# Reading back the last eight tiles of partial sums by gathers that leave out the tokens without a place, and summing the tiles in another order

## The reference, cut to what matters

```python
topk_w, topk_idx = jax.lax.top_k(scores, TOP_K)          # 6 experts for each of 2048 tokens
eid = topk_idx.reshape(-1)
order = jnp.argsort(eid)                                  # stable: by expert, then by token
pos = jnp.arange(T * TOP_K) - starts[eid_s]
valid = pos < CAP                                         # each expert takes its first 64 tokens
...
out_s = jnp.where(valid[:, None], d[eid_s, pos_c], 0.0)   # everything behind them gives 0
y = jnp.einsum('tkh,tk->th', out_exp.reshape(T, TOP_K, H), topk_w)
```

## Time and profile before

| | us |
|---|---|
| median of 3 runs | 652.74 |
| lowest and highest run | 652.25, 655.45 |
| profiled execution, its own time | 653.42 |
| span of its profile (first to last instruction) | 651.7 |
| pairs, from the first gather of rows to the last put's landing | about 501 to 620.4 |
| tail, from there to the end | 31.3 |

### The profile page before, as it was taken

How to read it: one execution, slowest core, us unless ns; L and a number is a source line. 1 busy time by engine, 2 the same in 40 slices (tenths; PEclk the granted TensorE clock), 3 DMA queues, 4 the chain that set the end, 5 groups by cost and what they waited for, 6 DMA issues and landing times.

```text
span 651.7 us, 7493 instructions
## 1 busy us (share of the span) xinstructions
PE 553.4 (85%) x2367; PEld 342.9 (53%) x2367; DVE 512.6 (79%) x1182; ACT 191.0 (29%) x372; POOL 126.2 (19%) x121
## 2 busy tenths in 40 slices
PE   7467999799999869999899776749889999999764
PEld 6344666444667456674566553427565444434443
DVE  7998888264899969999999999999988466456444
ACT  2113321225443254432643305421111333223100
POOL 2120201220001100011000210000001667677600
PEclk9679999987999959999899966789999999999979
DMA  7960000327301084010730207928561699995498
GB/s 273 409 213 34 33 1 34 113 65 259 130 0 49 26 310 153 0 42 25 277 113 1 81 25 260 384 78 307 175 230 55 198 341 352 344 312 87 55 342 310
DMA packets 62741, 105.75 MB, mean 162 GB/s; under 512 B 6096, under 2 KB 51920, under 8 KB 62192
## 3 DMA queue, kind: packets, MB, share of 16 engines
q1 hardware_dynamic: 51792, 85.97, 37.4%
q0 software_dynamic: 8608, 17.21, 10.2%
q10 hardware_dynamic: 2304, 2.10, 0.9%
HBM read 79.80 MB, written 25.46 MB: 162 GB/s over the span
## 4 chain that ended last, share of the span: by engine, by line
DVE 39%; PE 25%; DMA 17%; issue 5%; ACT 4%; POOL 2%; SPq 1%; DVEq 0%; POOLq 0%; ACTq 0%
DMA part_rows<-bc,att_s 12%; DVE scan_area L1370 10%; PE gate_ps L745 6%; PE up_ps L745 5%; DVE scan_area L1373 5%; DVE scan_area L1366 5%; PE misc_ps L762 4%; DMA bc<-part_rows 3%; DVE sig L1310 2%; PE turn_ps L678 2%; DMA front_area<-sorted_dram 1%; DVE work L1460 1%; DVE front_area L1315 1%; DVE ln_st L1123 1%; PE ssm_ps L699 1%
## 5 line engine op out<-in xcount | busy, mean ns | idle before, releaser
L1370 DVE TENSOR_TENSOR_SCAN scan_area<-scan_area 128x1024 f32<-128x1024 f32 x32 | 73.3, 2292 | 4.0 <-ACT scan_area L1044 0.5
L745 PE MATMUL gate_ps<-big,front_area 128*128 x144 | 72.8, 631 | 1.4 <-ACT front_area L944 1.4
L762 PE MATMUL misc_ps<-big,front_area 128*128 x288 | 67.5, 388 | 2.4 <-ACT front_area L944 2.4
L745 PE MATMUL up_ps<-big,front_area 128*128 x144 | 68.5, 598 | 0.0
L762 PEld LDWEIGHTS misc_ps<-big,front_area 128*128 128x128 f32 x288 | 55.0, 194 | 14.1 <-issue 6.7
L980 ACT ACTIVATE sig<-gate_ps 128x512 f32<-128x512 f32 (+1 forms) x48 | 28.5, 596 | 109.9 <-PE up_ps L745 79.4
L663 POOL DMA_INDIRECT part_rows<-bc,att_s x32 | 50.4, 1576 | 22.2 <-DMA part_rows<-bc,att_s 15.8
L1310 DVE SCALAR_TENSOR_TENSOR sig<-sig,gate_ps 128x512 f32<-128x512 f32 (+1 forms) x48 | 32.7, 682 | 23.2 <-ACT sig L980 22.8
L1044 ACT ACTIVATE scan_area<-scan_area,a_col 128x511 f32<-128x511 f32 x64 | 41.9, 714 | 31.0 <-DVE scan_area L1370 27.5
L745 PEld LDWEIGHTS up_ps<-big,front_area 128*128 128x128 f32 x144 | 28.2, 196 | 36.3 <-issue 36.3
L634 POOL DMA_INDIRECT front_area<-ysorted_dram,slot_idx x16 | 20.2, 1262 | 138.3 <-DMA ysorted_dram<-front_area 134.6
(11 more groups left out here) (276 smaller groups left out, 956.5 us busy)
## 6 DMA issues: line engine op xcount, KB each, us to landing
bc<-bc_dram SPq DMA_DIRECT2D x4, 4096.0 KB, 13.7
big<-in_wgu SPq DMA_DIRECT2D x14, 704.0 KB, 8.7
part_rows<-zeros SPq DMA_DIRECT2D x16, 512.0 KB, 15.4
front_area<-in_wgu SPq DMA_DIRECT2D x6, 704.0 KB, 7.6
scan_area<-in_wgu SPq DMA_DIRECT2D x6, 704.0 KB, 9.0
big<-part_rows SPq DMA_DIRECT2D x8, 512.0 KB, 6.4
big<-in_wd SPq DMA_DIRECT2D x12, 256.0 KB, 8.5
table<-row_area SPq DMA_DIRECT2D x4, 640.0 KB, 4.2
```

Source lines behind the costliest of these rows:

```text
L745: mm = pe.matmul(bank[:], xs_t[:, k, j, :], gu0[:, expert_of[b, j], k, g, half * 512:(half + 1) * 512], start=(k == 0), stop=(k == K - 1))
L762: mm = pe.matmul(misc_ps[:, 0:D], h0_t[:, half, c * P:(c + 1) * P], dn0[:, expert_of[b, j], half * 4 + c, :], start=(half == 0 and c == 0) ...
L1370: nc.vector.tensor_tensor_scan(buf.rearrange(flat), d_a[:, g % 2, :, :].rearrange(flat), buf.rearrange(flat), 0.0, ALU.mult, ALU.add).then ...
```

## The change

Four things, all for the end of the kernel.

1. **The last eight tiles** (8 to 15) are no longer loaded by SP. During the pairs, seven small DVE instructions and two of PE work out the highest token value in the list of places (`reach`: a row-wise maximum, a transpose, a maximum over the row, a product with ones that hands it to all partitions). From it comes, for each of the 1024 late tokens, an index: its own number, or its number plus 2048 where it lies behind the last token with a place. Behind its last put POOL issues eight indirect gathers (4 KB for a token), with `bounds_check=N - 1` and no error for an index beyond it, so that such a token isn't fetched.
2. Where nothing is fetched, the area must hold zeros: DVE clears the eight late areas, one 128x1024 memset in each of the pairs 23 to 30. `parts` is laid out anew, so that these areas are free by pair 23.
3. **The order of the sums**: DVE sums tiles 1, 3, 5, 7, 13, 14, 15, PE tiles 0, 2, 4, 6, 8, 9, 10, 11, 12. The stores follow in the order in which tiles are finished.
4. **WAKE_LAST**: 20 products of zeros on PE between the shared expert and the first sum.

```diff
+WAKE_LAST = 20
 TILES = B * J
+LATE = TILES // 2
+BY_PE = [0, 2, 4, 6, 8, 9, 10, 11, 12]
+BY_DVE = [1, 3, 5, 7, 13, 14, 15]
+OUT_ORDER = [i for two in zip(BY_DVE, BY_PE) for i in two] + BY_PE[len(BY_DVE):]
+CLEAR_FROM = PAIRS - LATE - 1
...
-        parts = [mem[:, n * part_size:(n + 1) * part_size] for mem, count in ((big, 8), (front_area, 5), (area, 3))
-                 for n in range(count)]
+        parts = [mem[:, at:at + part_size]
+                 for mem, base, count in ((big, 0, 4), (front_area, 2 * part_size, 4),
+                                          (big, 2 * pair_size, 6), (front_area, 0, 2))
+                 for at in range(base, base + count * part_size, part_size)]
...
-            for i in range(TILES):
+            for i in range(LATE):
                 sp.dma_start(parts[i], part_of[i]).then_inc(part_loaded[i], 16)
...
+            pool.wait_ge(reach_steps, 7)
+            pool.wait_ge(late_clear, LATE)
+            for put in rows_put:
+                pool.wait_ge(put, 16 * PAIRS // YO_RING)
+            for n in range(LATE):
+                pool.indirect_dma_start(parts[LATE + n], None, part_of_token,
+                                        bass.IndirectOffsetOnAxis(late_idx[:, n:n + 1], 0),
+                                        bounds_check=N - 1, oob_is_err=False).then_inc(part_loaded[LATE + n], 16)
...
+                if p == 5:
+                    pe.wait_ge(reach_steps, 2)
+                    pe.transpose(up_ps[0][0:1, 0:P], reach[:, 0:1], ident[:]).then_inc(reach_turned, 1)
+                if p == 9:
+                    pe.wait_ge(reach_steps, 3)
+                    pe.matmul(up_ps[0][:, P:P + 1], ones[0:1, :], reach[0:1, 1:2], start=True, stop=True
+                              ).then_inc(reach_turned, 1)
...
+            for _ in range(WAKE_LAST):
+                pe.matmul(turn_ps[0][:, 0:D], ident[:], zeros[:, 0:D], start=True, stop=True)
-            for i in range(0, TILES, 2):
+            for n, i in enumerate(BY_PE):
                 pe.wait_ge(part_loaded[i], 16)
...
+                if p == 11:
+                    dve.wait_ge(reach_turned, 2)
+                    ts(reach[:, 2:3], up_ps[0][:, P:P + 1], -1.0, float(PER_TOKEN * N), ALU.mult, ALU.add
+                       ).then_inc(reach_steps, 1)
...
+                if CLEAR_FROM <= p < CLEAR_FROM + LATE:
+                    dve.wait_ge(down1_filled, CLEAR_FROM - 1)
+                    nc.vector.memset(parts[LATE + p - CLEAR_FROM], 0.0).then_inc(late_clear, 1)
...
-            for i in range(0, TILES, 2):
-                part, xt = parts[i + 1], x_res[:, i + 1, :]
...
+            for n, i in enumerate(BY_PE):
+                if n < len(BY_DVE):
+                    part, xt = parts[BY_DVE[n]], x_res[:, BY_DVE[n], :]
```

More of the change, by code:

```diff
@@ L276, in build @@
         part_size = PER_TOKEN * D
-        parts = [mem[:, n * part_size:(n + 1) * part_size] for mem, count in ((big, 8), (front_area, 5), (area, 3))
-                 for n in range(count)]
+        parts = [mem[:, at:at + part_size]
+                 for mem, base, count in ((big, 0, 4), (front_area, 2 * part_size, 4),
+                                          (big, 2 * pair_size, 6), (front_area, 0, 2))
+                 for at in range(base, base + count * part_size, part_size)]
+        reached, reach, late = placed[:, 0:E], placed[:, E:E + 3], placed[:, E + 8:E + 8 + LATE]
+        late_idx = placed[:, E + 16:E + 16 + LATE].bitcast(U32)
         gate_ps = [ps("gate_ps0"), ps("gate_ps1")]
@@ L287, in build @@
         banks = (*gate_ps, *up_ps, *turn_ps, ssm_ps, misc_ps)
-        sum_ps = {i: banks[i // 2][:, 0:D] for i in range(0, TILES, 2)}
+        sum_ps = {i: banks[n % 8][:, n // 8 * D:(n // 8 + 1) * D] for n, i in enumerate(BY_PE)}
         sorted_dram = [nc.dram_tensor(f"sorted_dram{i}", (rows, D), F32).ap() for i, rows in enumerate((SLOTS, CHAIN))]
@@ L370, in build @@
         yo_halves = sem("yo_halves")
+        reach_steps = sem("reach_steps")
+        reach_turned = sem("reach_turned")
+        late_clear = sem("late_clear")
         rows_put = [sem(f"rows_put{i}") for i in range(YO_RING)]
@@ L925, in _ @@
                 shared_down(up_ps[h], h).then_inc(last_filled, 1)
-            for i in range(0, TILES, 2):
+            for _ in range(WAKE_LAST):
+                pe.matmul(turn_ps[0][:, 0:D], ident[:], zeros[:, 0:D], start=True, stop=True)
+            for n, i in enumerate(BY_PE):
                 pe.wait_ge(part_loaded[i], 16)
-                if banks[i // 2] in up_ps:
+                if banks[n % 8] in up_ps:
                     pe.wait_ge(last_added, 2)
+                if n >= 8:
+                    pe.wait_ge(out_ready, 2 * (n - 8) + 2)
                 for k in range(PER_TOKEN):
@@ L1103, in _ @@
             move_h1(PAIRS - 1)
-            for n, i in enumerate(i0 + half for i0 in range(0, TILES, 2) for half in (1, 0)):
+            for n, i in enumerate(OUT_ORDER):
                 act.wait_ge(out_ready, n + 1)
@@ L1539, in pair @@
                     weigh(p - 2)
+                if p == 3:
+                    stt(out=reached, in0=ids_t, scalar=float(PER_TOKEN * N), in1=ids_t, op0=ALU.is_lt, op1=ALU.mult
+                        ).then_inc(reach_steps, 1)
+                    dve.wait_ge(reach_steps, 1)
+                    reduce(reach[:, 0:1], reached, AX, ALU.max).then_inc(reach_steps, 1)
+                if p == 7:
+                    dve.wait_ge(reach_turned, 1)
+                    reduce(reach[0:1, 1:2], up_ps[0][0:1, 0:P], AX, ALU.max).then_inc(reach_steps, 1)
+                if p == 11:
+                    dve.wait_ge(reach_turned, 2)
+                    ts(reach[:, 2:3], up_ps[0][:, P:P + 1], -1.0, float(PER_TOKEN * N), ALU.mult, ALU.add
+                       ).then_inc(reach_steps, 1)
+                    dve.wait_ge(reach_steps, 4)
+                    ts(late, tok_value[:, LATE:TILES], reach[:, 2:3], float(N), ALU.is_lt, ALU.mult
+                       ).then_inc(reach_steps, 1)
+                    dve.wait_ge(reach_steps, 5)
+                    stt(out=late, in0=tok_value[:, LATE:TILES], scalar=-1.0 / PER_TOKEN, in1=late, op0=ALU.mult, op1=ALU.add
+                        ).then_inc(reach_steps, 1)
+                    dve.wait_ge(reach_steps, 6)
+                    ts(late_idx, late, float(N), None, ALU.add).then_inc(reach_steps, 1)
+                if CLEAR_FROM <= p < CLEAR_FROM + LATE:
+                    dve.wait_ge(down1_filled, CLEAR_FROM - 1)
+                    nc.vector.memset(parts[LATE + p - CLEAR_FROM], 0.0).then_inc(late_clear, 1)
             run_pairs(pair)
@@ L1549, in _ @@
             half = part_size // 2
-            for i in range(0, TILES, 2):
-                part, xt = parts[i + 1], x_res[:, i + 1, :]
[L1552 to L1558, removed]
+            for n, i in enumerate(BY_PE):
+                if n < len(BY_DVE):
+                    part, xt = parts[BY_DVE[n]], x_res[:, BY_DVE[n], :]
+                    dve.wait_ge(part_loaded[BY_DVE[n]], 16)
+                    tt(part[:, 0:half], part[:, 0:half], part[:, half:2 * half], ALU.add).then_inc(part_steps, 1)
+                    dve.wait_ge(part_steps, 2 * n + 1)
+                    tt(xt, xt, part[:, 0:D], ALU.add).then_inc(part_steps, 1)
+                    dve.wait_ge(part_steps, 2 * n + 2)
+                    tt(xt, xt, part[:, D:2 * D], ALU.add).then_inc(out_ready, 1)
+                dve.wait_ge(parts_summed, n + 1)
                 tt(x_res[:, i, :], x_res[:, i, :], sum_ps[i], ALU.add).then_inc(out_ready, 1)
```

1 line of the change is left out of this document (added).

## The result

The changed kernel takes 650.02 us (median of 17 runs, 648.26 to 653.53), the kernel before 653.69 in its 17 runs beside them (650.34 to 657.20). The ratio is 0.9955, with a 95% interval of 0.9937 to 0.9974: faster by 0.45%, 2.9 us (the ratio compares runs that stand beside each other; the two medians by themselves are 3.7 us apart). That is within the 0.5% that I had called "no change", and little more than half of the 5.2 us that I forecast.

A forecast was written before the change was run, and what follows sets the result against it. The prediction took DMA bytes to bound the tail; with 3.67 MB gone, PE's sums end last and the span falls from 651.7 to 646.5, memsets and wake-up costing 0: median 652.74 - 5.2 = 647.5 us, range 645.5 to 651.4.

The forecast's parts named there:

- no change: Whole kernel: a result within about 0.5%, 3.3 us, of the kernel before; chance 0.17.
- What bounds the tail: Tail: bytes set its end, 10.64 MB through full DMA engines at 416 GB/s, 1.57 us a tile.
- parts 1 and 3: Tail: 3.67 MB fewer loaded, POOL's gathers hidden, PE's sums end last at 644.2, span 646.5, 5.2 us less.
- The rule of the Trainium skill: Tail: two-SBUF-input DVE instructions contend with SBUF-reading GpSimd ones; four gathers could lose up to 0.69 us each, still hidden.
- part 2: Pairs: eight memsets of 0.95 us bring DVE to 2.95 of PE's 3.14 us and fit; cost 0.
- the slip of about 1 us: Pairs with memsets: slips of about 1 us where DVE catches up behind a landing, covered by the puts' slack.
- the memsets lengthen the pairs: Rival, pairs: each memset delays DVE and PE or holds POOL's puts; up to 4.2 of 5.2 us gone, 651.7; 7%.
- part 4: Ahead of the sums: 20 products, 8.7 us, end about tile 0's landing; 0 gained, 0.5 cost if pairs slip.
- the puts' 3.4 us in hand: Pairs: pair 29's put starts 3.4 us after its rows were weighed; DVE or PE work under that is hidden.
- the signs I had named: Trace: waits for tiles 8 to 15, a put over 1.6 us beside a memset, or first load behind 621.5 disprove steps.
- faster by over 0.5%: Whole kernel: a time below 649.5 us; chance 0.77.
- more tokens and slower gathers: Rivals, tail: places up to token 1500, 651.3 at most, 4%; gathers of 2 to 3 us, 649 to 652, 8%.

The follow-up runs named there:

- experiment 3: Changed kernel with the eight memsets moved behind DVE's last weighing and without the wake-up products; ratio to the kernel before 0.9934, tail 26.2 us.
- experiment 7: Kernel of experiment 3 with indices all inside the bound, so the gathers fetch all 1024 late tokens; ratio to the kernel before 1.0010, tail 31.2 us.
- experiment 2: Changed kernel without the 20 wake-up products; ratio to the kernel before 0.9935, tail 26.3 us.
- experiment 9: Kernel of experiment 3 with late tiles gathered in another order and summed between loaded ones, plus 18 wake-up products; ratio to the kernel before 0.9910, tail 24.0 us.
- experiment 4: Changed kernel without DVE's wait on down1_filled ahead of each memset; ratio to the kernel before 0.9963.
- experiment 5: Kernel before with only the eight memsets and their wait added in pairs 23 to 30; ratio to the kernel before 1.0014.
- experiment 10: Kernel of experiment 9 with tile 9 summed by DVE instead of PE; 645.70 us, ratio to the kernel before 0.9881, tail 24.0 us.

## Why the prediction was right or wrong

- **What bounds the tail**: right. Taking the bytes away takes 5.0 us off the tail, putting them back restores 31.2 (experiments 3 and 7).
- **Loads, gathers, sums** (parts 1 and 3): right. 3.6 MB fewer; gathers of 0.99 us for which nobody waited; with the disturbance gone, the last add ends 24.1 us behind the first load, for 23.7 in the sum. The rule of the Trainium skill that I weighed (SBUF — State Buffer, section "Who interferes with whom") changed nothing in the sum: in the changed kernel the eight gathers took 0.99 to 1.06. In experiment 2 one that began while an add with two SBUF inputs was under way (624.66 to 625.09) took 1.21, and in experiment 9 one that began with 0.58 us left of such an add took 1.44. One that began in the add of a PE sum, which reads one input from SBUF and one from PSUM (experiment 9, 0.26 us left), took 0.99. That agrees with the rule, with less than the 0.69 a piece I had allowed for.
- **The memsets** (part 2): this is the step that failed: DVE's round was taken too short, and the time that DVE needs to catch up was left out. I wrote "2.95 of 3.14: it fits". The row of a memset was sized right (0.91 for my 0.95), but 0.28 us of idle time come ahead of each, and the gaps between instructions weren't counted either; the round is 3.26. That is 0.12 above PE's round instead of 0.2 below it, but eight times 0.12 is only 1.0 us. The larger part is that DVE was late already when the memsets began, since a weighing had waited for a landing, and could no longer catch up: 26.0 us for eight rounds, against 22.4 before. Eight rounds of my 2.95 would have been 23.6, 1.2 more than before, which is the slip of about 1 us that I had granted; the 0.31 that each round is longer makes the other 2.5. I gave the rival "the memsets lengthen the pairs" 7%, with a price of 4.2 if all cover were gone; it is what happened, at about 0.9 us on the puts (with the scatter named above) and 7.0 on PE's last products. That the puts themselves aren't lengthened was right (1.58 us as before).
- **The wake-up** (part 4): "it could cost 0.5 if the pairs slip; not on the path either" was the second wrong step, and it hangs on the first. The slip for PE was not 1 us: counted from the put of pair 20, the shared expert ends after 26.8 us in the kernel before and after 33.8 in the changed one, 7.0 later. In experiment 4, where the clock stayed at 1.00, it is 30.2: 3.4 more by DVE's rounds. Of the remaining 3.6, 3.2 lie behind the 1.6 us wait, where only the clock differs (11.2 us from the last transposes to the shared expert's end, against 8.1). A chain of 8.7 us of filler work that ends just at a landing has no cover at all: it cost 1.7 us of the tail (experiment 2). I looked only at the puts' 3.4 us in hand, not at the last products of PE, for which there is no such cushion once filler stands behind them. Of the signs I had named, one came true in the changed kernel's trace: the first load at 621.8, behind 621.5.
- **The chances**: 0.77 on "faster by over 0.5%" rested on that step. The measured 650.02 lies in the range given (645.5 to 651.4), but that range was made for more tokens and slower gathers, neither of which came; that it holds a loss by the memsets is luck. The direction was right, the size wrong: 2.9 instead of 5.2.

## What to carry to other kernels

Compare rounds, not busy shares: work added to an engine that is busy for 2.0 of 3.14 us fits only if the whole round, with the gaps between the instructions, stays below. My round was 0.31 us too short, a tenth of it, so leave at least that. Where the engine must catch up behind a wait, its short rounds are in use as well: ask how late it is when the added work begins. Filler work for the clock is timed from where it begins: whatever delays its beginning puts all of it in front of the real work, so keep it off queues that can slip, or make it shorter than its gap by the slip. And put work that needs no landing between work that does: here the same bytes and the same sums in another order took the tail from 26.2 to 24.6, over a fifth of what all the changes took off it (31.2 to 24.0).

## What the runs showed of the hardware

- **Skipped rows are still packets.** The changed kernel's software queue has 9760 packets against 8608, 1152 more, 144 for each of eight gathers, as for a full one; packets under 512 bytes rose by 903 (6096 to 6999 on the pages), which is the number of late tokens behind 1144 (1151 - 1144 + 7 x 128). The bytes rose by 0.50 MB, 121 rows of 4 KB. A bound takes the bytes away, not the packet, nor POOL's time (0.99 us a gather; 1.01 in experiment 7, where all rows are fetched).
- **They don't land early.** Under full queues a gather of nothing but skipped rows landed with the traffic around it: 9.1 us behind the first load, and 6.2 behind its own start, for the second gather in experiment 9. With all rows fetched (experiment 7) a gather takes 10.3 to 15.0 us to land. The times in the changed kernel, tile 8's gather with 121 fetched rows among them:

```profile
DMA to landing us min/median/max: 5.2/7.9/8.4
```

- **A memset of 128x1024 takes 0.91 us on DVE**, each time the same, with 0.28 of idle time ahead of it behind a weighing and 0.16 behind another memset, where the other instructions of the round have 0.02 to 0.04. Removing its wait changes nothing.
- **The clock fell after PE had waited 1.6 us** at the end of rounds in which it had also waited, in the changed kernel and in experiments 2 and 5; in experiment 4, with the same 1.6, it was still at its upper level for the shared expert's products (5.37 us for the 24 steps), and in experiment 10 a wait of 2.05 us left it at 1.00. Which it will be can't be read from one wait.
- **A gather waits for the rest of an add with two SBUF inputs.** In the nine kernels with gathers on POOL, all ten that began with 0.18 us or more of such an add left took 1.05 to 1.44 us instead of 0.99. An add that began 0.04 us or more behind the gather didn't lengthen it.
